# Feed-forward with one rounding pass, expert weights split by GpSimd, output residual accumulated by TensorE

## The reference

```
h = relu(bitnet_linear([fused, avg_img], W_f1, b_f1))          # 256 -> 512
x = layernorm(x + bitnet_linear(h, W_f2, b_f2))                # 512 -> 128
# bitnet_linear: i_scale = max|x| / 127; qx = clip(round(x / i_scale), -128, 127)
#                qx @ ternary(W).T * (w_scale * i_scale) + b
for r in range(4):                                             # cur starts as x
    cw   = top-2 softmax weights of flat @ Wg[r] + bg[r]       # 4 experts
    hmid = gelu(flat @ W1[e] + b1[e]);  y = hmid @ W2[e] + b2[e]
    cur  = cur + sum_e cw[:, e] * y[e]
out = layernorm(x + cur)
```

## Time and profile before

| | us |
|---|---|
| median of 3 runs | 3006.16 (3005.99 to 3006.22) |
| profiled execution | 3004.93 |
| its span, first to last instruction | 3003.2 |
| mean granted TensorE clock | 0.879 of full speed |

### The profile page before, as it was taken

The page is one execution under the profiler, slowest core; times in us unless marked ns, Lnnn a source line. Parts: engine busy times, 40 slices in busy tenths (PEclk is TensorE's granted clock), DMA queues, the critical chain, the costliest instruction groups (busy, mean ns, idle before and its releaser), DMA issues. The chain is left out here.

```text
span 3003.2 us, 64102 instructions
## 1 busy us (share of the span) xinstructions
PE 2567.5 (85%) x17911; PEld 1559.4 (52%) x17911; DVE 2310.5 (77%) x6780; ACT 2294.5 (76%) x4463; POOL 519.4 (17%) x380
## 2 busy tenths in 40 slices
PE   2999999999999624866649999999999999999993
PEld 1777777777777613642324444444444444444442
DVE  3678677777777565778968888888888888888888
ACT  2778877887888534323449999999999999999992
POOL 2122322232222200100111111111111111111112
PEclk7789878887888755988779999999999999999995
DMA  2000000000000010000021111111111111121112
GB/s 74 13 17 15 11 10 16 15 10 10 17 15 10 16 26 1 0 0 0 0 56 43 52 47 47 51 44 54 42 56 42 56 42 56 42 56 42 56 42 70
DMA packets 182535, 95.98 MB, mean 32 GB/s; under 512 B 22539, under 2 KB 179291, under 8 KB 182491
## 3 DMA queue, kind: packets, MB, share of 16 engines
q1 hardware_dynamic: 182491, 95.45, 11.4%
HBM read 78.10 MB, written 4.73 MB: 28 GB/s over the span
## 5 line engine op out<-in xcount | busy, mean ns | idle before, releaser
L1815 DVE TENSOR_TENSOR c_Hl<-c_HF,c_Hh 128x512 f16<-128x512 f32 x1028 | 679.5, 688 | 158.8 <-ACT c_Hh L1703 141.4
L1699 ACT ACTIVATE c_HF<-c_H,c_b 128x512 f32<-128x512 f32 x1028 | 710.7, 691 | 65.6 <-PE c_H L1638 45.0
L1703 ACT ACTIVATE c_Hh<-c_H,c_b 128x512 f16<-128x512 f32 x1028 | 706.1, 687 | 0.0
L1753 POOL TENSOR_TENSOR c_EX<-c_euler,c_D 128x16 f32<-128x16 f32 x65 | 188.6, 2902 | 1211.6 <-DVE c_D L1788 1211.6
L1636 PE MATMUL c_H<-c_Ch,c_W1h 128*128 128x512 f16 x1028 | 390.2, 380 | 0.0
L1637 PE MATMUL c_H<-c_Cl,c_W1h 128*128 128x512 f16 x1028 | 390.1, 379 | 0.0
L1638 PE MATMUL c_H<-c_Ch,c_W1l 128*128 128x512 f16 x1028 | 390.0, 379 | 0.0
L1647 PE MATMUL c_Y<-c_Hh,c_W2h 128*128 128x512 f16 x1024 | 388.1, 379 | 0.6 <-DVE c_Hl L1815 0.6
L1648 PE MATMUL c_Y<-c_Hh,c_W2l 128*128 128x512 f16 x1024 | 388.1, 379 | 0.0
L1649 PE MATMUL c_Y<-c_Hl,c_W2h 128*128 128x512 f16 x1024 | 388.1, 379 | 0.0
L554 ACT ACTIVATE a_E<-a_T,a_nm 128x128 f32<-128x128 f32 x1024 | 331.2, 417 | 33.2 <-DVE a_nm L642 31.3
(11 more groups left out here) (286 smaller groups left out, 4257.7 us busy)
## 6 DMA issues: line engine op xcount, KB each, us to landing
c_CWB<-c_rows SPq DMA_DIRECT2D x260, 256.0 KB, 4.1
a_QN<-a_QH SPq DMA_DIRECT2D x128, 32.0 KB, 1.8
a_KN<-a_KH SPq DMA_DIRECT2D x128, 32.0 KB, 1.8
out<-d_O SPq DMA_DIRECT2D x16, 256.0 KB, 2.3
a_QN<-a_QL SPq DMA_DIRECT2D x64, 32.0 KB, 1.8
a_KN<-a_KL SPq DMA_DIRECT2D x64, 32.0 KB, 1.8
CUR<-in_ctx SPq DMA_DIRECT2D x1, 1848.0 KB
c_rows<-c_CWR SPq DMA_DIRECT2D x65, 8.0 KB, 1.4
```

The lines of the kernel that those rows point to most:

```text
L1699: act.activation(HF[:, k % 4, :], bH[k % 4][:, :], ACT.Gelu_apprx_tanh, bias=b1[:, g % EXPERTS, f:f + 1], scale=1.0 / WSCALE).then_inc(hf_ ...
L1703: act.activation(Hh[:, g % 2, f, :], bH[k % 4][:, :], ACT.Gelu_apprx_tanh, bias=b1[:, g % EXPERTS, f:f + 1], scale=1.0 / WSCALE).then_inc( ...
L1815: dve.tensor_tensor(Hl[:, g % 2, f, :], HF[:, k % 4, :], Hh[:, g % 2, f, :], ALU.subtract)\
```

## The change

- **Feed-forward.** The factor 1/scale is folded into ReLU's scale and bias once (hscale, hbias; ScalarE waits for them). One VectorE operation per chunk adds and subtracts MAGIC; the minimum of 127 is gone. GpSimd adds X and the bias b_f2 ahead of time into XF, which uses the space of T, and VectorE's one operation reads PSUM and XF. VectorE makes nb = -mean * rstd, and ScalarE normalizes (four activations of 128x128 per block, in place). GpSimd copies the result to X in place of ScalarE.
- **Expert weights.** A tile SH of 128x8192 f32 takes the place of the two KV tiles of the cross-attention and is passed to the experts' stage. SP loads W1 and W2 into it in the block of the search for the largest fused value; GpSimd scales, casts and subtracts in the next block. The experts' preparation keeps the router's Wg and b2. At the end of the experts SP waits for its last broadcast rows.
- **Output stage.** Four blocks in flight (DEPTH) and four PSUM banks. TensorE multiplies X by the identity into the bank, and transposes CUR on top of it. GpSimd makes the copies CB, two blocks ahead. VectorE makes statistics straight from PSUM (`sums`) and, one block later, nb = -mean * rstd (`offsets`). ScalarE normalizes from PSUM into O.

```diff
@@ experts' weights @@
+def expert_weights(SH):
+    n = EXPERTS * FFN
+    flat = SH[:, :]
+    half = flat[:, 2 * n:4 * n].bitcast(F16)
+    full = [flat[:, 0:n], flat[:, n:2 * n]]
+    high = [half[:, 0:n], half[:, n:2 * n]]
+    low = [half[:, 2 * n:3 * n], half[:, 3 * n:4 * n]]
...
+            @block.sync
+            def _(sp):
+                sp.dma_start(full[0]..., dr["W1"]...).then_inc(fetched, 16)
+                sp.dma_start(full[1]..., dr["W2"]...).then_inc(fetched, 16)
...
+            @block.gpsimd
+            def _(pool):
+                pool.wait_ge(fetched, 32)
+                for w in full:
+                    pool.tensor_scalar(w, w, WSCALE, 1.0, ALU.mult, ALU.mult).then_inc(parts, 1)
+                pool.wait_ge(parts, 2)
+                for w, hi in zip(full, high):
+                    pool.tensor_copy(hi, w).then_inc(parts, 1)
+                pool.wait_ge(parts, 4)
+                for w, hi, lo in zip(full, high, low):
+                    pool.tensor_tensor(lo, w, hi, ALU.subtract).then_inc(parts, 1)
+                pool.wait_ge(parts, 6)
...
-                parts = [(W1, W1h, W1l, 3), (W2, W2h, W2l, 4), (Wg, Wgh, Wgl, 3)]
+                parts = [(Wg, Wgh, Wgl, 3)]
@@ second feed-forward pass @@
                 with pool.Fori(0, NBLK // 2) as i:
                     for j in range(2):
+                        hold(pool, spare_pool, s_ok.sem, s_ok.at(i, j - 1))
+                        pool.tensor_tensor(XF[:, j, :, :], X[...], bf2_all[...], ALU.add).then_inc(xf_ok.sem, 1)
+                    for j in range(2):
                         pool.wait_ge(var_ok.sem, var_ok.at(i, j + 1))
                         pool.tensor_tensor(rstd[:, j, :], rstd[:, j, :], half[:, :], ALU.pow)
+                    for j in range(2):
+                        hold(pool, spare_pool, n_ok.sem, n_ok.at(i, j + 1))
+                        pool.tensor_copy(X[...], R[:, j, :, :]).then_inc(xw_ok.sem, 1)
...
                     relus(i, 1)
                     for j in range(2):
+                        act.wait_ge(nb_ok.sem, nb_ok.at(i, j + 1))
+                        for t in range(NB):
+                            last = act.activation(R[:, j, t, :], R[:, j, t, :], ACT.Identity,
+                                                  bias=nb[:, j, t:t + 1], scale=rstd[:, j, t:t + 1])
+                        last.then_inc(n_ok.sem, 1)
+                    for j in range(2):
                         act.wait_ge(t_ps.sem, t_ps.at(i, j + 1))
                         act.activation(CUR[...], bk[6 + j][:, :], ACT.Copy)
-                        act.activation(X[...], R[:, j, :, :], ACT.Copy).then_inc(xw_ok.sem, 1)
...
-                            dve.tensor_scalar(HR[...], HR[...], qi[:, 5:6], MAGIC, ALU.mult, ALU.add)
-                            dve.tensor_scalar(QH[...], HR[...], MAGIC, 127.0, ALU.subtract, ALU.min)
+                            dve.tensor_scalar(QH[...], HR[...], MAGIC, MAGIC, ALU.add, ALU.subtract)
...
+                        hold(dve, spare_dve, xf_ok.sem, xf_ok.at(i, n))
                         dve.wait_ge(y_ps.sem, y_ps.at(i, n))
-                        dve.scalar_tensor_tensor(r, bk[4 + j], sc[:, 6:7], bf2_all, ALU.mult, ALU.add)
-                        dve.tensor_tensor(r, r, X[...], ALU.add)
+                        dve.scalar_tensor_tensor(R[:, j], bk[4 + j], sc[:, 6:7], XF[:, j], ALU.mult, ALU.add)
...
-                        for t in range(NB):
-                            last = dve.tensor_scalar(R[:, j, t, :], R[:, j, t, :], mv[:, j, t, 0:1],
-                                                     rstd[:, j, t:t + 1], ALU.subtract, ALU.mult)
+                        dve.scalar_tensor_tensor(nb[:, j, :], mv[:, j, :, 0], -1.0, rstd[:, j, :],
+                                                 ALU.mult, ALU.mult).then_inc(nb_ok.sem, 1)
@@ output stage @@
+                with pe.Fori(0, NBLK // DEPTH) as i:
+                    for j in range(DEPTH):
+                        pe.wait_ge(n_ok.sem, n_ok.at(i, j + 1 - DEPTH))
+                        pe.matmul(bT[j][:, :], ident[:, :], X[...], start=True, stop=False)
                         pe.wait_ge(cb_ok.sem, cb_ok.at(i, j + 1))
                         for t in range(NB):
-                            last = pe.transpose(bT[j][...], CB[:, j, ...], ident[:, :])
+                            last = pe.matmul(bT[j][...], CB[:, j, ...], ident[:, :], start=False,
+                                             stop=t == NB - 1, is_transpose=True)
...
+                with pool.Fori(0, NBLK // DEPTH) as i:
+                    for j in range(DEPTH):
+                        hold(pool, spare_pool, t_ps.sem, ...)
+                        pool.tensor_copy(CB[...], CUR[...]).then_inc(cb_ok.sem, 1)
                         pool.wait_ge(var_ok.sem, var_ok.at(i, j + 1))
                         pool.tensor_tensor(rstd[:, j, :], rstd[:, j, :], half[:, :], ALU.pow)
...
+                    for j in range(DEPTH):
+                        sums(i, j)
+                        if j >= 1:
+                            offsets(i, j - 1)
+                    offsets(i, DEPTH - 1)
...
+                        act.wait_ge(nb_ok.sem, nb_ok.at(i, j + 1))
+                        act.wait_ge(stored[j].sem, stored[j].at(i, 0))
+                        for t in range(NB):
+                            last = act.activation(O[:, j, t, :], bT[j][...], ACT.Identity,
+                                                  bias=nb[:, j, t:t + 1], scale=rstd[:, j, t:t + 1])
```

More of the change, by code:

```diff
@@ L832, in _ @@
                 norm_step(NBLK - 1, k)
+ROUNDS, EXPERTS = 4, 4
+WSCALE = 256.0
+def expert_weights(SH):
[5 more added lines that the diff above has]
+    low = [half[:, 2 * n:3 * n], half[:, 3 * n:4 * n]]
+    return full, high, low
 CTX, DIN = 77, 96
@@ L842, with cross_attention_stage @@
 QUANT = ("d2v", "img", "txt", "att0", "att1", "f1", "f2")
-def cross_attention_stage(nc, held, dr, X, CUR):
+def cross_attention_stage(nc, held, dr, X, CUR, SH):
     used = []
@@ L895, in cross_attention_stage @@
         C = CUR[:, 0:B * DIN].rearrange("p (b d) -> p b d", b=B)
-        KV = [sb(f"KV{l}", [P, B, H // 2]) for l in range(2)]
+        KV = [SH[:, l * B * H // 2:(l + 1) * B * H // 2].rearrange("p (b d) -> p b d", b=B) for l in range(2)]
         avg = sb("avg", [P, B])
@@ new lines, in sums @@
+                def sums(i, j):
+                    dve.wait_ge(t_ps.sem, t_ps.at(i, j + 1))
+                    for t in range(NB):
+                        last = dve.bn_stats(st[:, j, t, :], bT[j][:, t * S:(t + 1) * S])
+                    last.then_inc(st_ok.sem, 1)
+                    hold(dve, spare_dve, st_ok.sem, st_ok.at(i, j + 1))
+                    for t in range(NB):
+                        last = dve.bn_aggr(mv[:, j, t, :], st[:, j, t, :])
+                    last.then_inc(mv_ok.sem, 1)
+                    dve.wait_ge(mv_ok.sem, mv_ok.at(i, j + 1))
+                    dve.tensor_scalar(rstd[:, j, :], mv[:, j, :, 1], 1e-5, None, ALU.add).then_inc(var_ok.sem, 1)
@@ new lines, in _ @@
+            @block.scalar
+            def _(act):
+                with act.Fori(0, NBLK // DEPTH) as i:
+                    for j in range(DEPTH):
+                        act.wait_ge(nb_ok.sem, nb_ok.at(i, j + 1))
+                        act.wait_ge(stored[j].sem, stored[j].at(i, 0))
+                        for t in range(NB):
+                            last = act.activation(O[:, j, t, :], bT[j][:, t * S:(t + 1) * S], ACT.Identity,
+                                                  bias=nb[:, j, t:t + 1], scale=rstd[:, j, t:t + 1])
```

169 lines of the change are left out of this document (79 added, 90 removed).

## The result

| | us | ratio to the kernel before [95% interval] |
|---|---|---|
| before, median of 4 runs | 3006.19 (3005.99 to 3010.74) | |
| after, median of 4 runs | 2960.77 (2956.79 to 2966.85) | 0.9847 [0.9824, 0.987] |
| after, profiled execution | 2964.35, span 2962.6 | |
| forecast | 2957.0 (2943 to 2981) | |

The change saves 45.4 us by the medians, where 49 were forecast. It is faster (the interval ends at 0.987), and the time lies in the range. The page of the changed kernel shows a wider spread of work: VectorE gave busy time to ScalarE and GpSimd, and the last slice of TensorE rose from 3 to 7 tenths, at clock 0.9 instead of 0.5.

What follows compares the result with a forecast made beforehand. TensorE bounds the untouched experts' stretch (1390 us); VectorE is busiest in most touched stages. Feed-forward -15, weights -15, search +2, output -21 sum to -49: 2955.9 profiled, 2957 us median; own range 2946 to 2967, overall 2943 to 2981.

Steps and rivals of the forecast that it cites:

- Feed-forward, -15: Second feed-forward pass: 2.15 us less per pair of blocks over seven distances, -15 us; ends -18.5 and -7.
- The circle through TensorE and ScalarE: Second feed-forward pass: down products, ReLUs, ScalarE's normalization and transposes set the pair's period, 13.5 us instead of 15.65.
- the same things stand: Second feed-forward pass: before the first and after the last pair nothing changes, so only seven distances between pairs gain.
- The cover for the adds: Second feed-forward pass: GpSimd's first residual-plus-bias add is ready 0.8 us before VectorE wants it.
- Weights, -15: Experts' preparation: small loads 6 us earlier and the split's 9 us off VectorE, together -15 us, range -10 to -16.
- The tie between SP's own issue and the large loads: Experts' preparation: small loads finish 6 us earlier without the large ones, or less if their 3.5 us is SP's issue time.
- Search pass, +2: Search for the largest hidden value: one GpSimd scaling between VectorE's two roundings costs +2 us, bounds 0 and +8.5.
- Output, -21: Output stage: statistics every 2.0 us per block in place of 3.5, -21 us; bounds -24 and -6 (2.9 per block).
- Rival B: Output stage: TensorE becomes the bound, 2.7 to 2.9 us per block in place of 2.0; 2969 us, chance 0.16.
- Rival C: GpSimd-VectorE port lock: search pass +8.5 in place of +2, output stage 0.6 us per block (9); 2972 us, chance 0.15.
- D: Experts' loop slows by late weight loads from its new tile: gain gone at 3.6% per chunk, 3022 us at 5%; chance 0.03.
- E: Second feed-forward pass: GpSimd delays the statistics, circle 15 us or more, -4 in place of -15; 2968 us, chance 0.06.

Runs made afterwards that it cites:

- experiment 4: Changed kernel with VectorE instead of ScalarE normalizing in the second feed-forward pass: 0.9827 of the kernel before; feed-forward 107.2 us instead of 115.9.
- experiment 6: Changed kernel with the two 1 MB weight loads issued again in the experts' preparation: 0.9865 of the kernel before; preparation 14.9 us instead of 7.6 to 8.1.
- experiment 2: Changed kernel plus an unneeded GpSimd reduction across partitions right behind the weight split: 0.9818 of the kernel before; until the reduction 2.9 us.
- Experiment 5: Changed kernel with every fourth block's offset also made after the next block's statistics, output stage: 0.9836 of the kernel before; output 39.1 us instead of 42.7.
- experiment 8: Changed kernel with four further edits, then GpSimd's feed-forward adds before its copies to X (0.9829 of the kernel before), or also those copies on ScalarE (0.9802).

## Why the prediction was right

- **The accounting.** The profiled time was forecast at 2955.9 and came at 2964.35, 8.4 us more: 2.4 from the stage nobody touched, 2.9 from the late reduction, 1.8 from the search pass, 1.2 from the feed-forward and 1.1 from the output stage; the short stretches and the preparation gave back 1.
- **Feed-forward, -15; measured -13.8.** The circle through TensorE and ScalarE was right step by step (13.5 us per pair; the down groups lie 13.5 apart on average). Two sizes in it were off and cancelled, which was luck: ScalarE's eight normalizations take 3.2 us instead of 2.5, the ReLUs start 0.2 us and end 0.4 us earlier. That this circle bounds the pair is shown by experiment 4, where shortening it by 1 us shortened the stage by 8.7. The seven distances gave (15.65 - 13.51) x 7 = 15.0 us, as forecast. The 1.2 missing lie behind the last pair, where "the same things stand" was wrong: from its first down product to the last copy it was 13.1 us and is 14.2, since ScalarE's normalization now stands ahead of the last transposes. It was not foreseen either that the first adds come late, 8.3 us of idle time behind the change of kind; that touches the first pair alone (its distance is 14.07 us, the others are 12.96 to 13.63). The cover for the adds, put at 0.8 us, held otherwise.
- **Weights, -15; measured -15.5.** Loads 6.6 us (forecast 6) and split 8.9 (forecast 9); experiment 6 gave back 6.8 to 7.3 for the loads alone. The 5.0 us that the small loads take were forecast as 1.5 + 3.5. The tie between SP's own issue and the large loads was decided for the large loads.
- **Search pass, +2; measured +3.8.** The mechanism was right and the size was not. The forecast price, one scaling between two roundings, was 1.7 us of it in fact, but on the tiny rounding and not between the long ones, because GpSimd started 7 us late. The rest is probably the one maximum beside a subtraction, which the sum had at nothing.
- **The step that was missing:** a reduction over partitions after 18 us of ordinary GpSimd work. Before, the last GpSimd work ahead of this reduction was the reduction of the fused maximum, with 60.4 us of idle time between them, so there was no change of kind. The next change, to the powers (queue entry at 1390.2), was hidden behind 13.2 us in which GpSimd waited for VectorE. So no row showed a price. It is 3 us here, shown by experiment 2.
- **Output, -21; measured -19.9.** Rival B fell: clock 1.00 and 1.12 us for the identity product, nearer to the key projection's 1.27 than to 2.07. The prediction put the 2.07 down to the backward read and kept it as a price apart from the clock; it was the clock, so B had one condition and not two. TensorE was busy 13.8 of the 19.0 us from 2936 to 2955, not nearly always, and kept 1.00. The end of -6 was also added up wrong: 14 x 0.9 us less gain than 21 is -8. A block is 2.06 us, close to the 2.0 forecast, but by luck and not for the reason given: VectorE's own work is 1.55 to 1.73 us per block (from statistics to statistics within a turn of four), and once in four it waits 1.06 us for the power and then 0.4 for GpSimd's copy (0.55 instead of 0.15). Experiment 5 took that away and gave 2.4 to 3.6 us.
- **Rival C, the lock,** was wrong in the output stage at its price (0.6 us per block) and right in kind: 0.4 us once in four blocks there, 1.7 and 2.5 us in the search pass, and the loss in experiment 8.
- **Rivals D and E** did not come: the experts' stretch is 1391.8 and 1391.9, and in the changed kernel the idle time ahead of a pair's first chain is TensorE's (25.5 us in 7 pairs); GpSimd delays the first pair alone.

## What to carry to other kernels

Work moved to an idle GpSimd is hidden in length but not at its edges: ask which VectorE operation it meets, and which of the two chains is the critical one, since either engine can be the one that waits for a whole instruction of the other. Give GpSimd's reductions over partitions a place of their own, or a dummy one early, because each change between them and scalings, adds or powers cost 5.5 to 8 us of its time here (copies did not). When an engine is relieved, lay out the circle of the next pair instruction by instruction with prices from rows: that gave 13.5 us against a measured 13.5, and it names which move pays next.

## What had not been expected of the hardware

- From GpSimd's queue entry to the first operation of the other kind: 6.9, 5.5 and 7.1 us in the changed kernel, in both directions, also where that kind had run before in the same kernel. Copies between two reductions brought no such entry.
- The same f32 product of 512 columns takes 2.07 us at granted clock 0.50 and 1.02 to 1.12 at 1.00, read forwards or, at 0.50, backwards.
- A 128x64 rounding of VectorE of 0.19 us took 1.90, a 128x8 maximum of 0.17 us took 2.63, while GpSimd worked on 128x2048 tiles.
- ScalarE's normalization of 128x128 with a column for bias and scale, from SBUF to SBUF, takes 0.40 us each in a run of eight (3.20 to 3.21); the exponentials of that shape take 0.32 each in a run of four.
- The same untouched 1046 us of code take between 1040.1 and 1052.7 us from one execution to the next.
